# Output projection inside the attention loop of a graph-and-mixer layer on one core

## The chip, the cores and the metric

The kernel runs on one core of one Trainium2 chip. The metric is the time of one execution in device microseconds. Before the change the median of three runs is 1399.31 us (1399.07 to 1401.28). Whatever is under 0.2% of that cannot be told from no change.

## The reference, cut to what matters

The input has 1250 rows of 512 numbers (padded here to ten tiles of 128 rows) and a list of 21250 edges. After a layer norm, three parts are added to the rows: a graph network with four experts, linear attention with eight heads, and a feed-forward network with sixteen experts. The change touches the attention, the gate of the graph experts, and the start of the graph's neighbour sums:

```
xn = layernorm(x)
gates = softmax(xn @ gate_W + gate_b); the two largest of 4 are chosen, with their gate values
q, k, v = split(xn @ w_qkv) into 8 heads of 64;  q, k = elu(q) + 1, elu(k) + 1
kv = sum over rows of k (x) v
z  = 1 / (q . sum over rows of k + 1e-6)
attention = (q @ kv * z) @ w_out + b_out
aggr = (sum of xn over the incoming edges) / in-degree
x = x + graph(xn, gates) + attention;  then x = x + ffn(layernorm(x))
```

## The kernel before, in words

Each engine runs one list of instructions in written order, and semaphores tie the lists together. TensorE is PE in the rows, VectorE is DVE, ScalarE is ACT, GpSimd is POOL, and SyncE (SP) issues most loads. An instruction that waits holds up all that is behind it on its engine.

The change lies in the first quarter of the run. In the order of TensorE this is:

1. Transposes of the normed rows (L1519), then transposes of edge data (L1526 to L1530).
2. The gate logits of all ten tiles (`B[6]`, L1537, recorded at L1509 since all products go through `product`), then three small products that bring the bounds of the edge windows to one row (L1541).
3. Twelve query products, three column chunks of about 426 times four pairs of heads. After the first TensorE waits for `ex_max`, the gate's maximum on VectorE (L1055). The edges are also turned into a table of counts `AT`, 32 columns (one window) at a time: VectorE makes one-hot matrices (`hot_pair`, 24 instructions for two windows, L1083 and L1084), TensorE multiplies them (`window_pair`, L1552), ScalarE copies the counts out (L761). There are twenty pairs; six stand among the query products, ten in the next stage, four among the output rows.
4. For each of ten tiles a K product, a V product and a window pair. ELU plus one is computed as max(x, 0) + min(exp(x), 1): one exponential on ScalarE, a minimum (L1077) and a combined maximum and add (L1078) on VectorE.
5. Four K-V sums over all rows, one per pair of heads (`B[6]`, `B[7]`). VectorE copies each out (L1109, L1110) into `KVB` and `KS`, the latter with eight columns, one per head.
6. Denominators of chunks 0 and 1 (`KS` by the queries), each followed on VectorE by an add and a reciprocal over 8 rows (L1115, L1116). Chunk 2 follows after loop step 1.
7. The attention loop, twelve steps. A step multiplies the queries by `KVB`, and broadcasts the reciprocals to the head's rows with the 8-row mask `heads`. ScalarE copies the broadcast out (`at_factor`, L798), VectorE multiplies (`at_whole`, L1136), ScalarE takes the high part (`at_high`, L787), and VectorE the low part (`at_low`, L1121).
8. Ten output rows, twelve products each (high and low parts by high and low weights). VectorE adds each to `X` (L1144). The weights `WO` are loaded when K and V are done, and split on ScalarE (L791) and VectorE (L1127).
9. The aggregation, ten tiles: counts to rows (`count_rows`, L1642), neighbour sums from high and low parts (`summed`, L1660), transposes (L1676). It waits for the residuals of all rows, for `XN_H` (ScalarE, L804) and `XN_L` (GpSimd, L585), and for counts copied by ScalarE (`aconv`, L835) after VectorE has signalled `at_ready` (L1173). Before this signal VectorE computes the ranks of the rows within their experts (L1149 to L1154).

Beside this, GpSimd adds the output bias to all ten tiles of `X` in one instruction (L580). VectorE goes from the gate's maximum straight on to softmax and choice (L1057 to L1072), and only then to the first one-hot matrices. Later stages (expert layers, slots, feed-forward) are not touched.

Of the kernel before, what the change touches and what calls it, by code (L numbers as in the profile page):

```python
# [23 lines left out]
ACT = mybir.ActivationFunctionType  # L24
# [56 lines left out]
def program(nc, x, src, dst, gate_w, gate_b, wl, bl, wr, w_qkv, w_out, b_out, ffn_gate, ffn_bias,  # L81
# [57 lines left out]
    KS = here("KS", [P, HP, 2 * HP], F32)  # L139
    heads = here("heads", [2 * HP, HP, P], F32)  # L140
    den = here("den", [2 * HP, NP], F32)
# [67 lines left out]
    place[0] = W20  # L209
    aconv = [here(f"aconv{i}", [P, NT, P], F32R) for i in range(2)]  # L210
    aconv_low = here("aconv_low", [P, NT, P], F32R)
# [63 lines left out]
    def sem(name):  # L275
# [6 lines left out]
        "q_pe", "q_exp", "q_done", "k_pe", "k_exp", "k_done", "v_pe", "v_done", "kv_pe", "kv_done",  # L282
# [240 lines left out]
    def _(pool):  # L523
        done = [0]

        def link(ins):
# [39 lines left out]
        link(pool.memset(heads[:, :, :], 1.0))  # L566

        link(pool.affine_select(out=heads[:, :, :], in_=heads[:, :, :], compare_op=ALU.is_ge, fill=0.0,
                                base=0, pattern=[[P, HP], [1, P]], channel_multiplier=-P // 2))
        link(pool.affine_select(out=heads[:, :, :], in_=heads[:, :, :], compare_op=ALU.is_ge, fill=0.0,  # L570
                                base=P // 2 - 1, pattern=[[-P, HP], [-1, P]], channel_multiplier=P // 2))
        pool.wait_ge(S["bounds_out"], 1)
        for h in range(HP):
# [4 lines left out]
        pool.wait_ge(S["small_in"], 16 * 3)  # L578
        pool.wait_ge(S["xn_done"], NT)
        pool.tensor_tensor(X[:, :, :], X[:, :, :], bo[:, :].unsqueeze(1).to_broadcast([P, NT, D]), ALU.add)\  # L580
            .then_inc(S["bias_added"], 1)
# [162 lines left out]
    def _(act):  # L744
# [9 lines left out]
        act.wait_ge(S["ex_max"], 1)  # L754
        act.activation(lg[:, :, 0:GE], lg[:, :, 0:GE], ACT.Exp).then_inc(S["ex_exp"], 1)

# [6 lines left out]

        for n in range(12):
            c, w = CHUNKS[n // KD]
            act.wait_ge(S["q_pe"], n + 1)
            if n >= 2:
                act.wait_ge(S["q_done"], n - 1)
            act.activation(expo[n % 2][:, 0:w], B[n % 2][:, 0:w], ACT.Exp).then_inc(S["q_exp"], 1)
            if n in PAIR_AFTER_Q:  # L770
                window_pair(PAIR_AFTER_Q[n])
        for i in range(NT):
# [5 lines left out]
            act.activation(expo[i % 2][:, :], B[2 + i % 2][:, :], ACT.Exp).then_inc(S["k_exp"], 1)  # L778
# [10 lines left out]
        act.wait_ge(S["kv_pe"], HP)  # L789
        act.wait_ge(S["wqkv_in"], 32)  # L790
        act.activation(WO[1][:, :, :], WO[0][:, :, :], ACT.Copy).then_inc(S["wo_h"], 1)  # L791
        for n in range(12):
# [6 lines left out]
            if n >= 1:  # L799
                at_high(n - 1)  # L800
        at_high(11)
        for n in range(NT):

            act.activation(XN_H[:, n, :], XN[:, n, :], ACT.Copy).then_inc(S["xn_h"], 1)  # L804
        for i in sorted(PAIR_AFTER_O):
            window_pair(PAIR_AFTER_O[i])
# [25 lines left out]
        act.wait_ge(S["o_pe"], NT)  # L832
# [140 lines left out]
    def _(dve):  # L973
# [8 lines left out]
        def normalise(dest, round):  # L982
# [18 lines left out]
            for i in range(NT):  # L1001
# [45 lines left out]
        dve.wait_ge(S["small_in"], 16 * 3)  # L1047
        dve.wait_ge(S["lg_pe"], NT)
        dve.wait_ge(S["mix_setup"], 1)
        link(dve.tensor_tensor(lg[:, :, 0:GE], B[6][:, 0:NT * GE].rearrange("p (t e) -> p t e", e=GE),  # L1050
                               gb[:, :].unsqueeze(1).to_broadcast([P, NT, GE]), ALU.add))
        link(dve.tensor_reduce(lt[:, 0, :], lg[:, :, 0:GE], AX.X, ALU.max))
        link(dve.tensor_tensor(lg[:, :, 0:GE], lg[:, :, 0:GE], lt[:, 0, :].unsqueeze(2).to_broadcast([P, NT, GE]),
                               ALU.subtract))
        dve.sem_inc(S["ex_max"], 1)  # L1055
        dve.wait_ge(S["ex_exp"], 1)
        link(dve.tensor_reduce(lt[:, 1, :], lg[:, :, 0:GE], AX.X, ALU.add))  # L1057
        link(dve.reciprocal(lt[:, 2, :], lt[:, 1, :]))
        link(dve.tensor_tensor(lg[:, :, 0:GE], lg[:, :, 0:GE], lt[:, 2, :].unsqueeze(2).to_broadcast([P, NT, GE]),
                               ALU.mult))  # L1060
        for i in range(NT):
            last = dve.max(top8[:, i, :], lg[:, i, :])
        link(last)
        for i in range(NT):
            last = dve.max_index(idx8[:, i, :], top8[:, i, :], lg[:, i, :])
        link(last)
        link(dve.tensor_copy(idxf[:, :, :], idx8[:, :, :]))
        for k in range(GSEL):
            link(dve.tensor_tensor(pick4[:, k, :, :], idxf[:, :, k:k + 1].to_broadcast([P, NT, GE]),
                                   io8[:, 0:GE].unsqueeze(1).to_broadcast([P, NT, GE]), ALU.is_equal))  # L1070
        link(dve.tensor_tensor(M4[:, 0:NT, :], pick4[:, 0, :, :], pick4[:, 1, :, :], ALU.add))
        link(dve.tensor_tensor(coef[:, :, :], M4[:, 0:NT, :], lg[:, :, 0:GE], ALU.mult))  # L1072


        def feature(n, dest, e_tile, bank, exp_sem, done_sem):
            dve.wait_ge(S[exp_sem], n + 1)
            link(dve.tensor_scalar(e_tile, e_tile, 1.0, None, ALU.min))  # L1077
# [18 lines left out]
        hot_pair(0)  # L1096
        for n in range(12):
            (c, w), j = CHUNKS[n // KD], n % KD
            feature(n, QT[:, j, c:c + w], expo[n % 2][:, 0:w], B[n % 2][:, 0:w], "q_exp", "q_done")
            if n in PAIR_AFTER_Q:  # L1100
                hot_pair(PAIR_AFTER_Q[n] + 1)
        for i in range(NT):
            feature(i, K[:, i, :], expo[i % 2][:, :], B[2 + i % 2][:, :], "k_exp", "k_done")
            hot_pair(PAIR_AFTER_KV[i] + 1)
        for h in range(HP):
            dve.wait_ge(S["kv_pe"], h + 1)
            b = B[6 + h % 2]
            for m, r in enumerate((slice(0, 64), slice(64, P))):
                dve.tensor_copy(KVB[r, h, r], b[r, r])  # L1109
                last = dve.tensor_copy(KS[r, h, 2 * h + m:2 * h + m + 1], b[r, P:P + 1])  # L1110
            last.then_inc(S["kv_done"], 1)
        def denominators(chunk):
            c, w = CHUNKS[chunk]
            dve.wait_ge(S["den_pe"], chunk + 1)
            link(dve.tensor_scalar(den[:, c:c + w], B[4 + chunk % 2][0:2 * HP, 0:w], 1e-6, None, ALU.add))  # L1115
            dve.reciprocal(den[:, c:c + w], den[:, c:c + w]).then_inc(S["den_done"], 1)  # L1116
# [7 lines left out]
        denominators(0)  # L1124
        denominators(1)
        dve.wait_ge(S["wo_h"], 1)
        dve.tensor_tensor(WO[2][:, :, :], WO[0][:, :, :], WO[1][:, :, :].bitcast(F32), ALU.subtract).then_inc(S["wo_l"], 1)  # L1127
        for n in range(12):
            (c, w), h = CHUNKS[n // HP], n % HP

            if n == HP:
                denominators(2)
# [4 lines left out]
            if n >= 1:  # L1137
                at_low(n - 1)
        at_low(11)
        for i in range(NT):  # L1140
            dve.wait_ge(S["o_pe"], i + 1)
            if i == 0:
                dve.wait_ge(S["bias_added"], 1)
            dve.tensor_tensor(X[:, i, :], X[:, i, :], B[4 + i % 2][:, :], ALU.add).then_inc(S["o_done"], 1)  # L1144
            if i in PAIR_AFTER_O and PAIR_AFTER_O[i] + 1 < NW // 2:
                hot_pair(PAIR_AFTER_O[i] + 1)


        link(dve.tensor_tensor(M4[:, 0:NT, :], M4[:, 0:NT, :], valid[:, :].unsqueeze(2).to_broadcast([P, NT, GE]), ALU.mult))  # L1149
        link(dve.memset(pref4[:, 0, :], 0.0))  # L1150
        for i in range(1, NT):
            link(dve.tensor_tensor(pref4[:, i, :], pref4[:, i - 1, :], M4[:, i - 1, :], ALU.add))
        link(dve.tensor_tensor(M4[:, NT, :], pref4[:, NT - 1, :], M4[:, NT - 1, :], ALU.add))
        dve.sem_inc(S["gm_sel"], 1)  # L1154
        dve.wait_ge(S["win_done"], NW)
        long = dve.value_load(bounds_i[0:1, LONG:LONG + 1], min_val=0, max_val=ETP)
        with dve.If(long > 0):
            more = dve.alloc_register("dve_more")
            dve.reg_mov(more, 1)
            with dve.Fori(0, NW) as w:  # L1160
                at = dve.value_load(bounds_i[0:1, bass.ds(w + NW, 1)], min_val=VISITS, max_val=ETP - 1)
                end = dve.value_load(bounds_i[0:1, bass.ds(w + 2 * NW, 1)], min_val=VISITS, max_val=ETP - 1)
                with dve.If(end > at):
                    with dve.Fori(at, end) as t:
                        m = dve.snap(more, min_val=1, max_val=NW * ET)
                        one_hots(0, 0, bass.ds(t, 1), bass.ds(w, 1)).then_inc(S["lhot_ready"], 1)
                        dve.wait_ge(S["long_pe"], m)
                        part = AT[:, :, bass.ds(w * WIN, WIN)]
# [783 lines left out]
```

## Time and profile before

| what | value |
|---|---|
| median of three runs | 1399.31 us |
| the profiled execution: time, span | 1401.73 us, 1400.0 us |
| busy: TensorE, VectorE, ScalarE, GpSimd | 1285.5, 709.7, 428.9, 251.5 us |
| mean granted clock of TensorE | 0.948 of full speed |
| busy TensorE within 210 to 245 us, clock | 34.99 us, 0.61 |

The rows that follow further down give busy time, waits, single instructions and the chain that ended last. Busy TensorE time is not peak work: at half clock (0.50 in the rows) the same product takes twice as long and the engine is as busy as before. A step of the chain of waits gives the time that the work took on the path, without its overlap with the next; these are the prices used. A float32 product shows as two instructions.

### The profile page before, as it was taken

The numbers are of one execution on the slowest core, as the hardware profiler recorded it, in microseconds if no ns is written. First come the engines' busy times: TensorE is split into PE (matmuls) and PEld (weight loads), VectorE is DVE, ScalarE is ACT, GpSimd is POOL, SyncE is SP. The second block draws the span as 40 slices with busy tenths as digits, with TensorE's granted clock in tenths as the row PEclk, the third lists the DMA queues.
The fourth block names the chain that finished last, engine by engine and source line by source line (L and its number), as shares of the span: only waits on it lengthen the run. The fifth ranks groups of instructions, "written<-read, shape, count | busy, mean of one in ns | idle before, by whom it ended". The sixth has DMA issues, their size and how long they took to land.

```text
span 1400.0 us, 20256 instructions
## 1 busy us (share of the span) xinstructions
PE 1285.5 (92%) x6004; PEld 984.1 (70%) x6005; DVE 709.7 (51%) x1884; ACT 428.9 (31%) x760; POOL 251.5 (18%) x295
## 2 busy tenths in 40 slices
PE   5799999989898998999899989598999999999994
PEld 4454452678786886888678868376877888887883
DVE  5797765747463354235422432646364455436552
ACT  2022212235343233224322322422252243225431
POOL 2300000304102201320132002202721111111111
PEclk8599996999998998999999999799999999999998
DMA  9500000063424423451333443205673355336522
GB/s 352 208 1 1 1 31 0 1 212 119 137 72 133 119 79 117 102 139 65 114 97 84 139 147 72 86 10 150 193 237 68 54 136 140 57 61 187 167 48 35
DMA packets 71812, 145.94 MB, mean 104 GB/s; under 512 B 11555, under 2 KB 12289, under 8 KB 71749
## 3 DMA queue, kind: packets, MB, share of 16 engines
q1 hardware_dynamic: 54212, 99.39, 21.0%
q0 software_dynamic: 17536, 45.77, 15.6%
q8 instruction: 32, 0.52, 0.2%
q14 instruction: 32, 0.25, 0.1%
HBM read 86.47 MB, written 58.67 MB: 104 GB/s over the span
## 4 chain that ended last, share of the span: by engine, by line
PE 67%; DMA 12%; DVE 7%; issue 7%; POOL 4%; ACT 1%; POOLq 1%; DVEq 1%; SPq 0%; ACTq 0%
PE B L1867 19%; PE B L1717 15%; PE B L1509 15%; PE B L1724 6%; DMA own<-hidden,idxO 5%; PE B L1660 3%; PE B L1803 3%; PE B L1552 2%; DMA xg<-slots 2%; POOL slots L712 1%; POOL chosen_ids L602 1%; PE B L1848 1%; PE B L1743 1%; DMA out_rows<-y,y_tok 1%; PE B L1909 1%
## 5 line engine op out<-in xcount | busy, mean ns | idle before, releaser
L1867 PE MATMUL B<-GUWH,xtH 128*128 (+1 forms) x344 | 145.0, 422 | 0.8 <-DVE xtL L1342 0.8
L703 POOL DMA_INDIRECT out_rows<-y,y_tok x44 | 68.6, 1558 | 380.0 <-ACT y L938 370.0
L1867 PE MATMUL B<-GUWL,xtH 128*128 (+1 forms) x344 | 136.7, 397 | 0.0
L1867 PE MATMUL B<-GUWH,xtL 128*128 (+1 forms) x344 | 136.6, 397 | 0.0
L1308 DVE SCALAR_TENSOR_TENSOR owtL<-B,owtH 128x512 fp32r<-128x512 f32 x21 | 14.5, 692 | 145.3 <-ACT owtH L863 145.3
L1084 DVE TENSOR_SCALAR key<-iota_key,keyT,neg_win 128x320 bf16<-128x320 int16 x240 | 87.8, 366 | 0.0
L1660 PE MATMUL B<-GH,conv 128*128 128x512 f32 x210 | 81.9, 390 | 0.0
L1660 PE MATMUL B<-GL,conv 128*128 128x512 f32 x210 | 81.8, 389 | 0.0
L1867 PE MATMUL B<-DNWH,htH 128*128 x176 | 75.3, 428 | 1.7 <-DVE htL L1342 1.7
L1867 PEld LDWEIGHTS B<-GUWH,xtL 128*128 128x128 f32 x344 | 65.1, 189 | 15.8
L1293 DVE TENSOR_TENSOR tr<-B,b 128x512 f32<-128x512 f32 x40 | 27.7, 691 | 92.6 <-PE B L1717 91.4
L1867 PEld LDWEIGHTS B<-GUWH,xtH 128*128 128x128 f32 x344 | 65.2, 190 | 12.6 <-DVE xtL L1342 0.9
L1867 PEld LDWEIGHTS B<-GUWL,xtH 128*128 128x128 f32 x344 | 65.3, 190 | 11.2
L1083 DVE TENSOR_SCALAR low<-iota_low,lowT 128x128 bf16<-128x128 int16 x240 | 61.0, 254 | 22.6 <-PE B L1552 21.4
L938 ACT ACTIVATE y<-B,y_gate 128x512 f32<-128x512 f32 x44 | 30.3, 689 | 135.4 <-PE B L1867 87.4
L822 ACT ACTIVATE hsXH<-XT 128x512 fp32r<-128x512 f32 x40 | 25.2, 631 | 150.5 <-PE B L1717 148.6
L1509 PE MATMUL B<-WQKV,XT 128*128 128x512 f32 x160 | 70.3, 592 | 0.0
L1867 PE MATMUL B<-DNWL,htH 128*128 x176 | 69.6, 395 | 0.0
L1867 PE MATMUL B<-DNWH,htL 128*128 x176 | 69.6, 395 | 0.0
L1803 PE MATMUL B<-ident,raw 128*128 128x128 f32 x432 | 64.5, 274 | 2.6 <-DVE DNWL L1342 1.5
L1717 PE MATMUL B<-W1H,hsXH 128*128 128x512 f32 x160 | 63.3, 396 | 2.8 <-DVE hsAL L1184 1.8
L1803 PEld LDWEIGHTS B<-ident,raw 128*128 128x128 f32 x432 | 52.6, 141 | 18.9 <-DVE DNWL L1342 3.6
(361 smaller groups left out, 2906.2 us busy)
## 6 DMA issues: line engine op xcount, KB each, us to landing
raw<-in_L_ffn_expert_gate_up SPq DMA_DIRECT2D x16, 1024.0 KB, 5.4
slots<-fill SPq DMA_DIRECT2D x5, 2112.0 KB, 19.6
hidden<-tr SPq DMA_DIRECT2D x40, 256.0 KB, 2.0
xg<-slots SPq DMA_DIRECT2D x34, 264.0 KB, 2.7
raw<-in_L_ffn_expert_down SPq DMA_DIRECT2D x8, 1024.0 KB, 5.7
counts<-astage SPq DMA_DIRECT2D x10, 648.0 KB, 3.1
W1R<-in_L_gnn_Wr SPq DMA_DIRECT2D x4, 1024.0 KB, 5.9
W1R<-in_L_gnn_Wl SPq DMA_DIRECT2D x4, 1024.0 KB, 8.8
```

What stands on the lines that cost most here:

```text
L703: pool.indirect_dma_start(out=out, out_offset=bass.IndirectOffsetOnAxis(ap=y_tok[:, 0:1], axis=0), in_=y[:, :], in_offset=None, compute_op ...
L938: act.activation(y[:, :], B[5][:, :], ACT.Copy, scale=y_gate[:, 0:1]).then_inc(S["y_done"], 1)
L1083: dve.tensor_scalar(low1[:, slot, v, :], iota_low[:, :], lowT[:, tile_col], None, ALU.is_equal)
L1084: return dve.tensor_scalar(key1[:, slot, v, :], iota_key[:, :], keyT[:, tile_col], neg_win[:, window], ALU.subtract, ALU.is_equal)
L1293: dve.tensor_tensor(tr[i % 2][:, :], B[2 - i % 2][:, :], b1[:, :], ALU.add).then_inc(S["t_done"], 1)
L1509: last = pe.matmul(bank, a, b, start=start and n == 0, stop=stop and n == len(todo) - 1)
L1552: last = pe.matmul(b, low1[:, lo_h, v, :], key1[:, lo_h, v, :], start=v == 0, stop=v == VISITS - 1)
L1660: last = pe.matmul(bank, counts[:, a, :], part[:, a, :], start=not begun and a == 0 and m == 0, stop=stop and a == NT - 1 and m == 1, skip ...
L1717: last = pe.matmul(B[2 - i % 2][:, :], rows[2 * (k // KD) + a][:, k % KD, :], W1[b][:, k, :], start=k == 0 and n == 0, stop=k == K2 - 1 an ...
L1724: last = pe.matmul(B[0][:, :], rows[a][:, k, :], W2[b][:, k0 + k, :], start=not begun and k == 0 and n == 0, stop=begun and k == KD - 1 an ...
L1803: last = pe.transpose(B[PREP_BANKS[q % PRING]][:, cols(k)], raw[:, q, cols(k)], ident[:, :])
L1867: last = pe.matmul(bank, rows[a][:, k, :], weights[b](k), start=k == 0 and n == 0, stop=k == KD - 1 and n == 2)
```

## The change

- The gate logits go into `B[5]` and stand among the query products, one tile after each of products 1 to 10; the window bounds come after product 0. The maximum follows the last query feature on VectorE. Its exponential on ScalarE follows the query features, softmax and choice follow output rows 6 and 7, and the ranks row 8.
- ELU plus one becomes max(x, 0) + exp(-relu(-x)): two passes on ScalarE (`below`) and one on VectorE.
- The bias is added by VectorE tile by tile between the copies of the K-V sums; the weight split moves there too.
- `KS` gets three shifted copies of its columns, so that all three chunks accumulate in one bank: 72 rows, chunk by chunk at rows 0, 32 and 64. One add and one reciprocal do for all; the mask `heads` has 72 rows and three versions, built by GpSimd when K and V are done, in the place of the query and key weights.
- Output rows 0 to 5 stand in the loop after steps 5, 6, 7, 9, 10 and 11. The last four window pairs stand after the denominators and after rows 1, 3 and 5; their one-hots on VectorE at steps 2, 7 and 10.
- `at_ready` is signalled before the last residual. The aggregation's first tile takes its sum before its counts, and waits for the residuals only after it.

```diff
-PAIR_AFTER_Q = {2 * p + 1: p for p in range(6)}
+PAIR_AFTER_Q = {2: 0, 4: 1, 6: 2, 8: 3, 10: 4, 11: 5}
-PAIR_AFTER_O = {2 * q + 1: 16 + q for q in range(4)}
+BIAS_AFTER_KV = ((0, 1, 2), (3,), (4, 5, 6), (7, 8, 9))
+PAIR_AFTER_O = {1: 17, 3: 18, 5: 19}
+PAIR_AFTER_DEN = 16
+O_AFTER = {5: 0, 6: 1, 7: 2, 9: 3, 10: 4, 11: 5}
+DEN = 72
...
+        pool.wait_ge(S["k_pe"], NT)
+        pool.wait_ge(S["v_pe"], NT)
+        link(pool.memset(heads[:, :, :, :], 1.0))
+        link(pool.affine_select(out=heads[:, :, :, :], in_=heads[:, :, :, :], compare_op=ALU.is_ge, fill=0.0,
+                                base=0, pattern=[[32 * P // 2, 3], [P, HP], [1, P]], channel_multiplier=-P // 2))
...
+        def below(dest, bank, n, done_sem):
+            act.activation(dest, bank, ACT.Relu, scale=-1.0).then_inc(S["ft_relu"], 1)
+            act.wait_ge(S["ft_relu"], n + 1)
+            act.activation(dest, dest, ACT.Exp, scale=-1.0).then_inc(S[done_sem], 1)
...
-        act.wait_ge(S["kv_pe"], HP)
         act.wait_ge(S["wqkv_in"], 32)
         act.activation(WO[1][:, :, :], WO[0][:, :, :], ACT.Copy).then_inc(S["wo_h"], 1)
+        window_pair(PAIR_AFTER_DEN)
...
+                of = 2 * h + m
+                last = dve.tensor_copy(KS[r, h, of:of + 2 * (DEN + 32) + 1:DEN + 32], b[r, P:P + 1].to_broadcast([64, 3]))
             last.then_inc(S["kv_done"], 1)
+            if h == 0:
+                dve.wait_ge(S["small_in"], 16 * 3)
+            for i in BIAS_AFTER_KV[h]:
+                last = dve.tensor_tensor(X[:, i, :], X[:, i, :], bo[:, :], ALU.add)
+            if h == 1:
+                dve.wait_ge(S["wo_h"], 1)
+                dve.tensor_tensor(WO[2][:, :, :], WO[0][:, :, :], WO[1][:, :, :].bitcast(F32), ALU.subtract)\
+                    .then_inc(S["wo_l"], 1)
...
+        dve.wait_ge(S["den_pe"], 1)
+        link(dve.tensor_scalar(den[:, :], B[5][0:DEN, 0:CHUNKS[0][1]], 1e-6, None, ALU.add))
+        dve.reciprocal(den[:, :], den[:, :]).then_inc(S["den_done"], 1)
...
+        hot_after = {2: 17, 7: 18, 10: 19}
         for n in range(12):
...
             if n >= 1:
                 at_low(n - 1)
+            if n - 1 in O_AFTER:
+                residual(O_AFTER[n - 1])
+            if n in hot_after:
+                hot_pair(hot_after[n])
         at_low(11)
+        gating = {6: gate_softmax, 7: gate_choice, 8: expert_ranks}
+        for i in range(O_AFTER[11], NT):
+            residual(i)
+            if i in gating:
+                gating[i]()
...
+        for chunk, (c, w) in enumerate(CHUNKS):
+            for h in range(HP):
+                last = pe.matmul(B[5][0:DEN, 0:w], KS[:, h, chunk * DEN:(chunk + 1) * DEN], QT[:, h, c:c + w],
+                                 start=chunk == 0 and h == 0, stop=chunk == 2 and h == HP - 1, skip_group_check=True)
+        last.then_inc(S["den_pe"], 1)
+        window_pair(PAIR_AFTER_DEN)
...
+            if n == 0:
+                pe.wait_ge(S["mix_setup"], 2)
+                pe.wait_ge(S["den_done"], 1)
+            product(B[2 + n % 2][:, 0:w], [(heads[:, n // HP, h, :], den[:, 0:w])]).then_inc(S["at_pe"], 1)
+            if n in O_AFTER:
+                output_rows(O_AFTER[n])
...
         for i in range(NT):
-            count_rows(i)
+            if i == 0:
+                pe.wait_ge(S["conv_done"], 1)
+            else:
+                count_rows(i)
...
+            if i == 0:
+                pe.wait_ge(S["o_done"], NT)
+                count_rows(0)
+            else:
                 transpose_rows_out(i - 1)
```

## Rows read from the trace of the kernel before

**Rows 1.** Chain of waits, 0 to 360 us: start, length, engine, line, count.
```profile
66.07 8.30 PE B L1509 x16
74.37 1.63 PE B L1552 x12
76.00 5.72 PE B L1509 x16
...
105.39 6.87 PE B L1509 x16
...
271.61 5.52 PE B L1509 x24
...
284.35 0.69 DVE X L1144
...
290.20 2.39 PE B L1642 x10
292.59 6.28 PE B L1660 x20
298.87 1.07 PE B L1642 x10
299.94 4.64 PE B L1660 x20
```

**Rows 2.** Stretches: length, busy PE, PEld, DVE, ACT, POOL; then clock, DMA, GB/s.
```profile
36.00:41.00 5.00, 5.00 (x28) 4.90 (x28) 0.00 (x0) 0.00 (x0) 0.00 (x0) 0.50 1.06 388
74.00:83.00 9.00, 9.00 (x41) 5.23 (x39) 7.77 (x30) 2.89 (x6) 0.00 (x0) 1.00 0.01 2
206.83:210.48 3.65, 3.65 (x9) 1.18 (x9) 3.62 (x3) 0.53 (x1) 0.00 (x0) 1.00 0.00 0
217.00:244.00 27.00, 27.00 (x33) 7.79 (x32) 12.25 (x19) 7.79 (x16) 0.00 (x0) 0.51 0.00 0
```

**Rows 3.** Timeline of all engines, 0 to 70 us: start, length, engine, line, operation.
```profile
11.08 0.62 POOL L570 TENSOR_SCALAR_AFFINE_SELECT heads<-heads 8x512 f32<-8x512 f32 x1
...
24.79 15.85 PE L1509 MATMUL B<-gw,XT 128*128 128x4 f32 x80
...
28.65 0.15 DVE L1037 TENSOR_TENSOR lohi<-lohi 40x1 f32<-40x1 f32 x1
...
43.17 10.96 POOL L580 TENSOR_TENSOR X<-X,bo 128x5120 f32<-128x5120 f32 x1 [0.25 <-POOL V L574]
43.57 10.62 DVE L1053 TENSOR_TENSOR lg<-lg,lt 128x40 f32<-128x40 f32 x1
```

**Rows 4.** Waits of TensorE, 0 to 365 us: total, times, longest.
```profile
PE B L1509 <- DVEq L1055: 7.3, 1, 7.3
PE B L1642 <- ACT aconv L835: 5.9, 1, 5.9
```

**Rows 5.** The load of the query, key and value weights: issue and landing.
```profile
L394 SPq DMA_DIRECT2D WQKV<-in_L_mix_w_qkv x1: 480/480/480, 6.2 to 6.2; - x1
...
DMA to landing us min/median/max: 14.6/14.6/14.6
```

**Rows 6.** Timeline of VectorE, 186 to 300 us.
```profile
189.69 0.25 DVE L1083 TENSOR_SCALAR low<-iota_low,lowT 128x128 bf16<-128x128 int16 x1 [2.12 <-PE B L1552]
...
194.93 0.20 DVE L1109 COPY KVB<-B 64x64 f32<-64x64 f32 x1
...
204.70 2.82 DVE L1116 RECIPROCAL den<-den 8x428 f32<-8x428 f32 x1
...
210.74 2.22 DVE L1127 TENSOR_TENSOR WOL<-WO,WOH 128x2048 fp32r<-128x2048 f32 x1
...
253.16 1.38 DVE L1084 TENSOR_SCALAR key<-iota_key,keyT,neg_win 128x320 bf16<-128x320 int16 x1
```

**Rows 7.** Timeline of TensorE: the denominators of chunks 0 and 1.
```profile
201.00 5.90 PE L1509 MATMUL B<-QT,KS 128*8 128x428 f32 x16 [0.69 <-DVE KS L1110]
```

**Rows 8.** Timeline of GpSimd: the low parts of the normed rows.
```profile
246.89 12.54 POOL L585 TENSOR_TENSOR XN_L<-XN,XN_H 128x512 fp32r<-128x512 f32 x10 [192.75 <-ACT XN_H L804]
```

More of the change, by code:

```diff
@@ L565, in _ @@
         link(pool.memset(KS[:, :, :], 0.0))
[L566 to L571, printed above, removed]
         pool.wait_ge(S["bounds_out"], 1)
@@ L576, in _ @@
         pool.sem_inc(S["mix_setup"], 1)
[L578 to L581, printed above, removed]
+        pool.wait_ge(S["k_pe"], NT)
[3 more added lines that the diff above has]
+                                base=0, pattern=[[32 * P // 2, 3], [P, HP], [1, P]], channel_multiplier=-P // 2))
+        link(pool.affine_select(out=heads[:, :, :, :], in_=heads[:, :, :, :], compare_op=ALU.is_ge, fill=0.0,
+                                base=P // 2 - 1, pattern=[[-32 * P // 2, 3], [-P, HP], [-1, P]],
+                                channel_multiplier=P // 2))
+        pool.sem_inc(S["mix_setup"], 1)
         for i in range(NT):
@@ L1109, in _ @@
                 dve.tensor_copy(KVB[r, h, r], b[r, r])
-                last = dve.tensor_copy(KS[r, h, 2 * h + m:2 * h + m + 1], b[r, P:P + 1])
+                of = 2 * h + m
+                last = dve.tensor_copy(KS[r, h, of:of + 2 * (DEN + 32) + 1:DEN + 32], b[r, P:P + 1].to_broadcast([64, 3]))
             last.then_inc(S["kv_done"], 1)
[L1112 to L1116, printed above, removed]
+            if h == 0:
[6 more added lines that the diff above has]
+                    .then_inc(S["wo_l"], 1)
+        last.then_inc(S["bias_added"], 1)
         def at_low(n):
@@ new lines, in windows_done @@
+        def windows_done():
+            dve.wait_ge(S["win_done"], NW)
+            with dve.If(long > 0):
+                more = dve.alloc_register("dve_more")
+                dve.reg_mov(more, 1)
+                with dve.Fori(0, NW) as w:
+                    at = dve.value_load(bounds_i[0:1, bass.ds(w + NW, 1)], min_val=VISITS, max_val=ETP - 1)
+                    end = dve.value_load(bounds_i[0:1, bass.ds(w + 2 * NW, 1)], min_val=VISITS, max_val=ETP - 1)
+                    with dve.If(end > at):
+                        with dve.Fori(at, end) as t:
+                            m = dve.snap(more, min_val=1, max_val=NW * ET)
+                            one_hots(0, 0, bass.ds(t, 1), bass.ds(w, 1)).then_inc(S["lhot_ready"], 1)
+                            dve.wait_ge(S["long_pe"], m)
+                            part = AT[:, :, bass.ds(w * WIN, WIN)]
+                            dve.tensor_tensor(part, part, B[6][:, 0:WC].rearrange("p (a w) -> p a w", a=NT), ALU.add)\
+                                .then_inc(S["long_done"], 1)
+                            dve.wait_ge(S["long_done"], m)
+                            dve.reg_add(more, more, 1)
+            dve.sem_inc(S["at_ready"], 1)
@@ new lines, in expert_ranks, with residual @@
+        def expert_ranks():
+            link(dve.tensor_tensor(M4[:, 0:NT, :], M4[:, 0:NT, :], valid[:, :].unsqueeze(2).to_broadcast([P, NT, GE]), ALU.mult))
+            link(dve.memset(pref4[:, 0, :], 0.0))
+            for i in range(1, NT):
+                link(dve.tensor_tensor(pref4[:, i, :], pref4[:, i - 1, :], M4[:, i - 1, :], ALU.add))
+            link(dve.tensor_tensor(M4[:, NT, :], pref4[:, NT - 1, :], M4[:, NT - 1, :], ALU.add))
+            dve.sem_inc(S["gm_sel"], 1)
+        def residual(i):
+            if i == NT - 1:
+                windows_done()
+            dve.wait_ge(S["o_pe"], i + 1)
+            if i == 0:
+                dve.wait_ge(S["bias_added"], 1)
+            dve.tensor_tensor(X[:, i, :], X[:, i, :], B[4 + i % 2][:, :], ALU.add).then_inc(S["o_done"], 1)
@@ L1149, in _ @@
[L1149 to L1168, printed above, removed]
-                        dve.tensor_tensor(part, part, B[6][:, 0:WC].rearrange("p (a w) -> p a w", a=NT), ALU.add)\
-                            .then_inc(S["long_done"], 1)
-                        dve.wait_ge(S["long_done"], m)
-                        dve.reg_add(more, more, 1)
@@ L1652, in count_rows @@
                 for a in range(NT):
-                    one(aconv_low, a, False)
+                    last = one(aconv_low, a, False)
+                if i == 0:
+                    last.then_inc(S["ag_low_pe"], 1)
             one(aconv[i % 2], NT - 1, True).then_inc(S["ar_pe"], 1)
```

161 lines of the change are left out of this document (76 added, 85 removed).

## The prediction

> **What bounds the kernel now.** I read the page, then the busy time by stage, the waits of TensorE, the timeline of all engines at the start, and the chain of waits. Everything that the change touches lies before the second aggregation tile, whose products start at 299.94 us [rows 1]; what follows only moves along. TensorE is the bound almost throughout: in the query stage it is busy 9.00 of 9.00 us at clock 1.00 [rows 2]. Three places lose time. The gate logits, 80 instructions with 4 moving columns, take 15.85 us at the start, at clock 0.50 [rows 2, 3]. Then TensorE waits 7.3 us for VectorE's gate maximum [rows 4]: its subtract of 128x40 shows 10.62 us, inside GpSimd's one bias add of 10.96 us [rows 3]. In the attention loop TensorE is busy 27.00 of 27.00 us, but at clock 0.51 [rows 2]. And after the last output row it waits 5.9 us for the count copies [rows 4].
>
> **Query stage.** Before, the first logit starts at 24.79 and K's first product at 105.39 [rows 1, 3]: 80.6 us. The weights for the queries were issued at 6.2 and landed 14.6 us later [rows 5], so the first query product can start at 24.9, where the logits stood. Its work: 12 query products at 5.72/2 us, 34.3; six window pairs at 1.63, 9.8 [rows 1]; 80 logit instructions; 0.5 us for the window bounds. A logit costs between 0.107 us (ten short matmuls in 1.07 us [rows 1]) and 0.20 (15.85/80 [rows 3]); I take the first, 8.6 us in all, because pairs mixed with query products ran at clock 1.00 [rows 2]. Waits: the bounds are ready at 28.8 [rows 3], product 0 ends at 27.7, so 1.1 us. The first hot pair, 5.24 us on VectorE [rows 6], starts only after feature 1, about 35.3, and ends at 40.6; TensorE arrives at 36.8 and needs 1.63 us, so 2.3 are lost, and 0.6 more at the last pair. The sum is 57.2 us: K starts at 82.1, 23.3 us earlier. Logits, their maximum and the bias leave the path; ScalarE's second pass per feature (some 0.6 us, 22 times) and VectorE's lost minimum both lie beside TensorE, whose nine-microsecond period leaves either slack. The K and V stage keeps its 8.5 us per tile. Two waits for the maximum are new: V's second product, and ScalarE's list, where K's exponentials stand behind it. The maximum follows a hot pair and a feature on VectorE, near 88.8; V's second product comes at 94.0, and K's first feature, late by 3.5 us, lets the next hot pair end at 96.8, before TensorE wants it at 97.5. Both are hidden, the second by 0.7 us.
>
> **K-V sums and denominators.** What is late next is VectorE. Its last hot pair moves from 189.69 to 166.4 and would end at 171.6. But GpSimd now builds the head mask there, three operations over 3x512 elements, about 1.2 us ahead of it. One over 512 took 0.62 us [rows 3], so they take 1.9 us (by the instruction) to 5.6 (by the element), and a hot-pair operation beside a GpSimd operation took 1.38 us instead of about 0.3 [rows 6]. The delay is 0.7 to 4.4 us; I take 3.4, nearer the price by element. Behind it VectorE must pass sixteen small copies (some 0.15 us each, 2.4), seven of the ten bias adds (0.6 each, by the 0.69 of a like row [rows 1]: 4.2) and the weight split (2.22 [rows 6]) before TensorE has its last key sum: the denominators start at 183.8, not 201.00 [rows 7]. The pauses are too short for what is put into them, 6.1 of the 23.3 us go here. Then come 24 instructions at 5.90/16 (8.8 us [rows 7]) and one window pair: the loop starts at 194.2, before at 206.9 (201.00 plus 5.90). One add of 0.6 and one reciprocal of 2.82 us [rows 6] end at 196.1, so the first broadcast waits 1.0 us. The two other reciprocals were hidden; the third denominator product, 3.0 us, leaves the loop.
>
> **Loop and output rows.** Work: 12 steps at 1.83 us (two in 3.65 us at full clock [rows 2]), 22.0; ten rows at 5.52/2, 27.6; three pairs, 4.9 [rows 1]. VectorE now has hot pairs among the loop's products. At step 2 the pair stands before product 3, which step 5 needs: VectorE is done 7.9 us after step 2, TensorE has 3.66 us to do, so 4.3 lost. At step 7 row 3 needs a low part behind the pair: 9.0 against 6.4, 2.6 lost. At step 10 row 6: 10.2 against 9.0, 1.2 lost. With the 1.0 above that is 63.6 us: the last row ends at 257.8. Before it took from 206.9 to 284.35 [rows 1].
>
> **Start of the aggregation.** GpSimd's low parts (12.54 us [rows 8]) start with row 6, and the gate's choice now stands on VectorE beside them. An operation with two SBUF inputs waits there like the 10.62 us one [rows 3]; with five such the low parts end 13.5 us after row 6 began, row 9 11.0 after. Only then come the last but one residual, the expert ranks and the copy, the 5.9 us chain of before [rows 4]. The gap is 8.4 us; without holding, 2.8. Then the first tile's sum, its counts, a new wait of 1.3 us (its counts must be copied out before the next counts, which the sum covered before) and 1.07: 4.64 + 1.07 + 1.3 + 1.07, plus the 3.0 us of cold clock that the same start cost before (2.39 + 6.28 against 1.07 + 4.64 [rows 1]). The second tile starts at 277.2 instead of 299.94: 22.7 us.
>
> GpSimd's list now waits for K and V ahead of the mask; behind it stand only the low parts, wanted 70 us later. SP's loads and stores wait for the same rows and come earlier by as much; the load of the output weights has over ten microseconds of room.
>
> **The clock.** Right after a paced hot pair two query products took 8.30 us instead of 5.72 [rows 1]: 2.6 us. The first pair stays paced, so I charge this again, and half of it, 1.3, at the denominators, where TensorE idles some 7 of 11 us: 22.7 less 3.9 is 18.8. The profiled run took 1401.73 us, 1400.0 of it span, and is 2.4 above the median; taken from each it leaves 1382.9 for a run like it and 1380.5 for the median.
>
> **Two rules of the Trainium skill.** That GpSimd holds VectorE is seen in the 10.62 and 1.38 us rows [rows 3, 6]. The Trainium skill, SBUF — State Buffer, section SBUF: two separate sides, says the port pair is locked for a whole instruction, also by an operation that only writes; no row here shows the latter. By it the mask's fill holds VectorE too, and the 3.4 us stay; by rows alone two of three operations would hold it, some 1.2 us less. The other: the loop was busy throughout and yet at 0.51 [rows 2]. The Trainium skill, TensorE: Matmul & The Clock Gate, Part 1, says that sustained activity releases the slow clock and idling brings it back; by that rule alone the loop would have been fast before, so the trace disagrees, and the new mask with 72 rows instead of 8 need not decide it as the rule would have it.
>
> **Rivals.** First, the clock is low longer. For: the loop's pattern was granted 0.51. A step at half clock costs 27.00/33x4, 3.3 us, 1.4 more. Until row 0 that is six steps, less the two hidden in the 4.3 us wait: 5.7 us, 1386.2. If instead query products 0 to 2 and their logits run at half, that is 10.3 us more, of which the waits of 1.1 and 2.3 and the 2.6 already charged take up 6.0: 4.3, 1384.8; both, 1390.5. Against: the first two steps after the denominators ran at full clock [rows 2], and output rows follow from step 5. Second, GpSimd holds VectorE little (short mask operations, gate operations slipping between): 2.7 and 5.6 us back, 1372.2, and without the cold spells 1368.3. Against: the 10.62 us row. Third, slower: the logits, which ran at 0.50, keep the clock at half through the whole query stage. Its 52.7 us of work double, K starts near 127 instead of 105.4, 22 us late; with the other parts, which about cancel, 1422. It decides once half clock covers more than about 22 of the 52.7 us beyond the forecast. Against: window pairs among query products ran at 1.00. The change not doing what it says: if the query weights came late the first product could not move up, but they landed at 20.8.
>
> **Chances.** My sum 0.52; clock low longer 0.27; little holding 0.14; slower 0.05; a gain eaten up by several of these, 0.02. Range 1368 to 1392, which takes in the first two rivals; the last two cases lie outside. A measurement of this kernel tells about 0.2% from no change. Faster by more 0.92, within 0.03, slower 0.05.
>
> **What would show it.** Right: K's first product near 82; a VectorE hot pair stretched beside GpSimd's mask; denominators near 184, loop near 194, one wait of about 4 us at step 5; a gap of 8 us before the aggregation; its second tile near 280. Wrong: a clock of 0.5 over most of the query stage or the loop; gate operations at 0.2 us beside the low parts; denominators before 180.

## The result and the profile after

The changed kernel takes 1378.94 us (median of four runs, 1377.66 to 1379.18), the kernel before took 1400.3 on the same chip: on record as a ratio of 0.9861, 95% interval 0.984 to 0.9883 (the quotient of the two medians, 0.9847, lies inside it). Forecast were 1380.5 us, and 1382.9 for a run like the profiled one; the profiled run took 1379.03 us, 1377.3 of it span, 22.7 less than before.

The chain of waits of the changed kernel, 0 to 360 us (start, length, engine, line, count), answers to [rows 1]:

```profile
82.63 6.87 PE B L1538 x16
...
184.30 10.52 PE B L1628 x24
...
259.55 1.23 DVE pick L1101
...
263.50 0.69 DVE X L1182
267.13 1.17 ACT aconv L843
268.34 7.35 PE B L1700 x20
...
277.98 1.30 PE B L1680 x10
279.29 4.60 PE B L1700 x20
```

K's first product starts 22.8 us earlier than before, the denominators 16.7, the second aggregation tile 20.65. The first scatter of the chosen rows starts 20.67 us earlier, so the gain reaches the next stage whole. Of the other 2.0 us that the profiled run gained, 1.5 come where the list of chosen rows is loaded back (5.48 us, before 7.01); the change does not touch that load.

TensorE's waits of the changed kernel, 0 to 350 us (total, times, longest), answer to [rows 4]:

```profile
...
PE B L1700 <- ACT aconv L843: 6.4, 1, 6.4
PE B L1538 <- DVE expo L1190: 4.7, 1, 4.7
PE B L1538 <- DVE QL L1138: 4.2, 2, 3.1
PE B L1628 <- DVE KS L1123: 3.6, 1, 3.6
PE B L1538 <- DVE KS L1123: 2.7, 1, 2.7
...
PE B L1538 <- DVE den L1143: 1.3, 1, 1.3
PE B L1680 <- ACT astage L849: 1.2, 1, 1.2
PE B L1572 <- DVEq L1046: 1.0, 1, 1.0
```

The 7.3 us wait for the gate's maximum is gone. All waits listed are new or moved. Each of them but the one of 1.3 us shrank or went in one of the experiments, the one of 1.0 us only with the logits in a block. The stretches of the changed kernel, with the columns of [rows 2] (the clock is the third number from the end):

```profile
25.00:42.00 17.00, 15.13 (x65) 8.33 (x66) 12.04 (x49) 4.13 (x8) 0.59 (x4) 1.00 1.06 385
42.00:82.00 40.00, 39.88 (x193) 25.63 (x191) 30.15 (x125) 13.59 (x27) 0.00 (x0) 1.00 0.31 113
...
184.30:188.50 4.20, 4.20 (x7) 1.56 (x8) 1.87 (x3) 0.00 (x0) 0.00 (x0) 0.59 0.00 0
...
210.10:216.00 5.90, 5.87 (x12) 3.75 (x13) 2.63 (x5) 1.53 (x3) 0.00 (x0) 0.52 0.00 0
216.00:230.00 14.00, 14.00 (x58) 9.28 (x56) 6.53 (x21) 3.57 (x8) 0.00 (x0) 1.00 0.00 0
...
233.20:236.30 3.10, 3.10 (x8) 2.48 (x9) 1.55 (x3) 0.02 (x1) 0.00 (x0) 0.52 0.00 0
...
268.40:274.00 5.60, 5.60 (x14) 4.39 (x15) 0.00 (x0) 1.05 (x1) 0.04 (x1) 0.52 1.05 399
```

The query stage is at full clock, and so is the loop apart from short stretches. Each stretch near 0.5 (1.2 of 2.4 GHz), called a cold stretch in what follows, stands behind one of the waits above: the 3.6, the 4.7, the 3.1 and the 6.4 us one. Before, the clock was low in 27 us of uninterrupted work.

### The profile page after: what moved, and what is told of

It is laid out like the page before. It is cut to its first block, busy times and chain, and to the rows that moved or that the text cites. A ratio compares the mean times of both kernels' runs of the same rounds, so it can differ in the third digit from the quotient of the medians.

```text
span 1377.3 us, 20264 instructions
## 1 busy us (share of the span) xinstructions
PE 1255.1 (91%) x6004; PEld 975.5 (71%) x6005; DVE 693.8 (50%) x1868; ACT 441.2 (32%) x782; POOL 243.8 (18%) x294
## 4 chain that ended last, share of the span: by engine, by line
PE 64%; DMA 12%; DVE 9%; issue 7%; POOL 4%; ACT 1%; DVEq 1%; POOLq 1%; SPq 0%; ACTq 0%
PE B L1919 19%; PE B L1769 15%; PE B L1538 10%; PE B L1776 6%; DMA own<-hidden,idxO 5%; PE B L1700 4%; PE B L1855 3%; DMA xg<-slots 2%; PE B L1584 2%; POOL chosen_ids L606 1%; POOL slots L716 1%; PE B L1900 1%; PE B L1795 1%; DMA out_rows<-y,y_tok 1%; DVE key L1063 1%
## 5 line engine op out<-in xcount | busy, mean ns | idle before, releaser
L831 ACT ACTIVATE hsXH<-XT 128x512 fp32r<-128x512 f32 x40 | 25.3, 631 | 149.0 <-PE B L1769 147.1
```

## The experiments

Each edit starts from the changed kernel unless the text says otherwise. The runs stood on other chips, beside the kernel before (1396.8 to 1397.8 us there) but not beside the changed kernel. So ratios to the kernel before are compared with 0.9861, and stages by the trace. Each kernel has one trace.

**Logits in a block.**

```diff
+        for i in range(NT):
+            gate_logits(i)
+        window_bounds()
         for n in range(12):
...
-            elif n <= NT:
-                gate_logits(n - 1)
```

> The changed kernel with its 80 logit instructions back in one block, ahead of the first query product, and the window bounds right behind them; the maximum stays behind the last query feature. Theory: a block of short products runs at half clock (0.56 in that stretch before) and hands the low clock on. The block takes 15.85 us instead of 10 times 0.81 among the query products, the 1.0 us wait for the bounds goes: K's first product moves from 82.5 to 89 if full speed is back at once, and towards 95 if the first query products also run slow, as before (5.98 us against 3.14). Time 1386 to 1391. Rival: what made the logits slow was the load beside them or the wait for the maximum, not their standing together; then the block takes some 8 us, K starts near 82, 1378.

1389.21 us, ratio 0.9943 (0.9926 to 0.996), about 11 us more. Timeline of TensorE, then the first stretch:

```profile
25.23 14.87 PE L1538 MATMUL B<-gw,XT 128*128 128x4 f32 x80
...
40.52 11.05 PE L1538 MATMUL B<-XT,WQKV 128*128 128x428 f32 x24
...
93.12 7.03 PE L1538 MATMUL B<-WQKV,XT 128*128 128x512 f32 x16
```
```profile
25.00:41.00 16.00, 16.00 (x92) 15.80 (x92) 3.86 (x16) 0.00 (x0) 0.00 (x0) 0.59 1.06 385
```

The same 80 instructions cost 8.1 us among the query products and 14.87 in a block, and three products behind the block take 11.05 us, where a product takes 3.14 at full clock. K starts 10.6 us later. The load beside them is as heavy in both kernels (385 GB/s) and TensorE does not wait for the maximum here, so the rival falls.

**The maximum early, then with a long GpSimd operation.** Both start from the kernel with the block of logits.

```diff
         for n in range(12):
...
+            if n == 0:
+                gate_maximum()
...
             if n == 0:
...
+                pe.wait_ge(S["ex_max"], 1)
...
+        pool.tensor_tensor(X[:, :, :], X[:, :, :], fill[:, 0:D].unsqueeze(1).to_broadcast([P, NT, D]), ALU.add)\
+            .then_inc(S["bias_added"], 1)
```

> The kernel with the logits in one block, and the gate's maximum ahead of the first query feature, TensorE waiting for it before its second query product, as before; the bias stays on VectorE in ten adds late. Theory: the 7.3 us wait of before was GpSimd's one add holding the maximum, not the maximum: it takes some 2 us beside a product at half clock of 6 us, so no wait over 0.5 us comes back: 1388 to 1391, as with the logits in a block alone. Rival: the wait belongs to the maximum's chain itself, and 5 to 7 us come back: 1394 to 1397.

> The same, and GpSimd adds a row of zeros to all ten tiles in one operation where it added the bias before. Theory: the maximum's subtract waits for the end of that add, and TensorE waits some 7 us before its second query product; the clock stays low for longer: K's first product moves to where it was before, 103 to 106: 1396 to 1400. Rival: the two do not hold each other; then 1388 to 1391.

1390.69 us, ratio 0.9946 (0.9924 to 0.9967), and 1398.74 us, ratio 1.0012 (1.0002 to 1.0023). TensorE waits for the maximum behind its first query product. The last two lines of the edit are the second kernel's alone; `fill` holds zeros. The subtract of the maximum, in the timelines of VectorE of the first and of the second kernel, with GpSimd's add and TensorE's wait in the second:

```profile
43.50 0.20 DVE L1081 TENSOR_TENSOR lg<-lg,lt 128x40 f32<-128x40 f32 x1
```
```profile
43.48 10.65 DVE L1085 TENSOR_TENSOR lg<-lg,lt 128x40 f32<-128x40 f32 x1
...
43.11 10.96 POOL L577 TENSOR_TENSOR X<-X,fill 128x5120 f32<-128x5120 f32 x1 [0.25 <-POOL V L572]
```
```profile
PE B L1544 <- DVEq L1087: 7.2, 1, 7.2
```

The maximum itself was harmless: alone the subtract takes 0.20 us and TensorE does not wait; beside the add it takes 10.65, and a wait of 7.2 us is back. That add costs 8 us. Together with the block of logits it moves K's first product from 82.5 to 102.0 us, 19.5 of the 22.8 us that the change won there; the rest was not taken apart.

**Mask of 8 rows.**

```diff
-            product(B[2 + n % 2][:, 0:w], [(heads[:, n // HP, h, :], den[:, 0:w])]).then_inc(S["at_pe"], 1)
+            product(B[2 + n % 2][:, 0:w], [(heads[0:2 * HP, 0, h, :], den[0:2 * HP, 0:w])]).then_inc(S["at_pe"], 1)
```

> The changed kernel with only 8 rows of mask and reciprocals in each broadcast product, those of the first column chunk for all (so the attention of the other chunks is scaled by wrong reciprocals). Theory: the 1.83 us of a step before came with the operand of 8 rows, and 72 rows took it away: a step (two products) goes from 1.45 back to 1.83 us at full clock, twelve times, of which about four lie in waits for VectorE: plus 3 us, 1382; if the clock then also falls to half as it did before, a step takes 3.4 us and it is 1385 to 1395. Rival: the height is nothing, the steps were slow because the third denominator and the later reciprocals lay among them: steps stay at 1.45 us, 1379.

1390.68 us, ratio 0.9954 (0.9937 to 0.997). This total can't be read: the changed attention sent rows to other experts, and the feed-forward network ran one tile more (45 against 44). The loop can. Timeline of TensorE, then three stretches:

```profile
201.84 0.98 PE L1538 MATMUL B<-den,heads 8*128 8x428 f32 x2
...
203.67 0.98 PE L1538 MATMUL B<-den,heads 8*128 8x428 f32 x2
204.58 1.40 PE L1538 MATMUL B<-QT,KVB 128*128 128x426 f32 x2
```
```profile
199.00:204.50 5.50, 5.50 (x13) 1.77 (x12) 2.73 (x5) 2.48 (x5) 0.00 (x0) 1.00 0.01 3
204.50:213.90 9.40, 6.58 (x9) 1.79 (x8) 7.46 (x29) 2.06 (x4) 0.00 (x0) 0.53 0.00 1
...
218.70:234.00 15.30, 14.75 (x54) 8.01 (x53) 8.04 (x28) 4.09 (x9) 0.00 (x0) 1.00 0.00 0
```

A step is back at 1.83 us at full clock (201.84 to 203.67), as in [rows 2], and the clock falls at 204.6, in the midst of work without a wait, while the changed kernel stays at 1.00 through the same steps (199.0 to 204.5). So the height of the operand sets the price of a step, and in this trace 8 rows brought the low clock. They did not keep it: from 218.7 on, with output rows between the steps, the clock is back at 1.00. In the kernel before no output rows stood between the steps and the clock stayed low for 27 us. The change put 72 rows and output rows into the loop together, and 72 rows without the output rows were not run, so their shares are not known. From the first broadcast to the first sum this kernel takes 73.1 us (198.22 to 271.32), the changed one 69.9. What in the hardware makes it so, no run shows.

**Bias adds and weight split behind the last copy; mask behind it.** Two kernels; the last three lines are the second one's, and the split moves in the first like the adds.

```diff
-            for i in BIAS_AFTER_KV[h]:
-                last = dve.tensor_tensor(X[:, i, :], X[:, i, :], bo[:, :], ALU.add)
...
+        for i in range(NT):
+            last = dve.tensor_tensor(X[:, i, :], X[:, i, :], bo[:, :], ALU.add)
...
-        pool.wait_ge(S["k_pe"], NT)
-        pool.wait_ge(S["v_pe"], NT)
+        pool.wait_ge(S["kv_done"], HP)
```

> The changed kernel with the ten bias adds and the weight split behind the last copy of the K-V sums instead of between the copies. Theory: they stand in TensorE's way there. The third sum still waits for the hot pair, the denominators start at 181.4 instead of 184.3, the idle time before them shrinks from 3.6 to under 1 us, and with it the stretch at half clock behind it (1.7 us) may go; VectorE has 8.6 us of work beside 8.85 us of denominators: 1374 to 1376. Rival: the work does not fit there, the add and the reciprocal come later by what the denominators come earlier: 1379.

> The changed kernel with GpSimd building the mask only after the last copy of the K-V sums. Theory: the mask held VectorE: the hot pair goes from 8.05 back to 5.24 us, and the denominators start 2.8 us earlier, near 181.5: 1376; the mask is ready near 187, before the loop. Rival: VectorE's delay was made up in the waits behind it; the denominators move by less than 1 us: 1379.

1376.21 us, ratio 0.9853 (0.9837 to 0.987), and 1375.54 us, ratio 0.985 (0.9834 to 0.9867): each ratio lies within the interval of the changed kernel's, so the totals tell nothing and the traces decide. Denominators in the timeline of TensorE of the changed kernel, of the first and of the second; then the last two K-V sums and the denominators of the kernel with the mask of 8 rows, whose instructions are those of the changed kernel up to the loop:

```profile
184.30 10.51 PE L1628 MATMUL B<-QT,KS 128*72 128x428 f32 x24 [3.61 <-DVE KS L1123]
```
```profile
180.57 8.81 PE L1626 MATMUL B<-QT,KS 128*72 128x428 f32 x24 [0.70 <-DVE KS L1123]
```
```profile
183.05 8.81 PE L1627 MATMUL B<-QT,KS 128*72 128x428 f32 x24 [3.61 <-DVE KS L1122]
```
```profile
177.11 6.38 PE L1538 MATMUL B<-V,K 128*128 128x129 f32 x40 [2.73 <-DVE KS L1123]
...
185.76 8.81 PE L1628 MATMUL B<-QT,KS 128*72 128x428 f32 x24 [2.28 <-DVE KS L1123]
```

From the first K-V sum to the start of the denominators the changed kernel takes 16.1 us (168.21 to 184.30), the first kernel 12.9 (167.71 to 180.57), the second 13.3 (169.80 to 183.05): 3.2 and 2.8 us of waiting are won, and both rivals fall. The 1.7 us of low clock in the denominators go as well, but they cannot be put down to the edits: with the mask of 8 rows the same work shows them too at 8.81 us, since there the cold stretch falls on the last two sums (6.38 us, in the changed kernel 5.05), ahead of a wait that hides it. So from the first sum to the first broadcast the unedited stage takes 30.2 or 28.5 us, the edited ones 25.3 and 25.7. In the second kernel the hot pair is back at 0.25 us for an operation [rows 6], the wait of 2.7 us is gone, while the 3.6 us wait stays and yet the clock does not fall: in this trace that wait by itself did not bring the low clock. What decides where a cold stretch falls, no run shows.

**One-hots of pair 17 at step 5.**

```diff
-        hot_after = {2: 17, 7: 18, 10: 19}
+        hot_after = {5: 17, 7: 18, 10: 19}
```

> The changed kernel with the one-hots of pair 17 made on VectorE at step 5 of the loop, when output rows follow, and no longer at step 2. Theory: the 4.7 us wait of step 5 comes from their place alone, and the 5.9 us at clock 0.52 behind it come from that wait. Both go, the pair's product finds its one-hots ready behind row 1: 4.7 and some 2.8 us, 1371.5. Rival: VectorE is late in the loop as a whole, the wait comes back before pair 17 or row 1, and 1 to 3 us are won: 1376 to 1378.

1370.87 us, ratio 0.9801 (0.9777 to 0.9825), 8 us less. Waits of TensorE:

```profile
PE B L1538 <- DVE QL L1138: 4.8, 3, 3.1
...
PE B L1584 <- DVE key L1063: 0.4, 1, 0.4
```

The 4.7 us wait is gone, 0.6 (in the first line, 4.2 before) and 0.4 came for it, and the clock stays at 1.00 behind step 5. From the first broadcast to the first sum it takes 63.0 us against 69.9.

**Gate in VectorE's pauses.**

```diff
+        gating = {2: gate_softmax, 4: gate_choice, 6: expert_ranks}
         for i in range(NT):
...
+            if i in gating:
+                gating[i]()
             hot_pair(PAIR_AFTER_KV[i] + 1)
```

> The changed kernel with softmax, choice and expert ranks in VectorE's pauses at K and V tiles 2, 4 and 6, not behind output rows 6 to 8. Theory: beside GpSimd's low parts each of these operations waits for one of them, and their chain makes the gap of 6.4 us before the aggregation. Without them the residual of row 8 follows its row, and the low parts end last, 1.3 us after the last row; the cold start of the first sum (7.35 us against 4.6) goes with the gap if the clock fell for its sake: 5 to 8 us, 1371 to 1374. The pauses hold them: a tile has 2.4 us of VectorE idle. Rival: they do not fit there, pairs of the K and V stage come late and take back 2 to 4 us; or the gap stays over 5 us since the low parts themselves are held.

1372.39 us, ratio 0.9818 (0.9797 to 0.9838), 6 us less. Timeline of TensorE and of GpSimd:

```profile
264.77 0.47 PE L1700 MATMUL B<-XN_H,aconv 128*128 128x512 f32 x1 [1.58 <-POOL XN_L L589]
...
252.07 12.55 POOL L589 TENSOR_TENSOR XN_L<-XN,XN_H 128x512 fp32r<-128x512 f32 x10 [79.48 <-ACT XN_H L815]
```

The gap is 1.6 us, not 6.4, and no wait came in the K and V stage. The low parts take 12.55 us with nothing of the gate beside them, as with it (12.54): the time that the two held each other was VectorE's alone. The first sum ran at full speed; the next tile was the slow one, so not the whole cold start was won.

**Counts first.**

```diff
             if i == 0:
-                pe.wait_ge(S["conv_done"], 1)
-            else:
-                count_rows(i)
+                pe.wait_ge(S["o_done"], NT)
+            count_rows(i)
...
-            if i == 0:
-                pe.wait_ge(S["o_done"], NT)
-                count_rows(0)
-            else:
+            if i >= 1:
                 transpose_rows_out(i - 1)
```

> The changed kernel with the aggregation's first tile in the old order: its counts before its sum, both behind the residuals. Theory: the new order wins nothing here and adds a wait of 1.2 us between the first two tiles, since the gap ends with the copy of the counts in either case: from the end of the gap to the second tile's sum 9.7 us (as before) instead of 10.9, 1377.7. Rival: the new order is needed, because the last residual comes later than the copies; then the old one starts up to 1 us later.

1376.09 us, ratio 0.985 (0.9829 to 0.987). Chain of waits:

```profile
266.64 1.17 ACT aconv L843
...
277.38 4.64 PE B L1700 x20
```

From the copy to the second sum it takes 10.7 us, in the changed kernel 12.2, and the wait of 1.2 us between them is gone. By the traces this part of the change lost 1.4 us; by time alone it can't be told from nothing.

**ELU as before.**

```diff
-            act.activation(dest, bank, ACT.Relu, scale=-1.0).then_inc(S["ft_relu"], 1)
...
+            act.activation(dest, bank, ACT.Exp).then_inc(S[done_sem], 1)
...
+            link(dve.tensor_scalar(e_tile, e_tile, 1.0, None, ALU.min))
```

> The changed kernel with ELU plus one as before: one exponential on ScalarE, a minimum and a combined operation on VectorE. Theory: the one pass and the other both lie beside TensorE, whose tiles of 8.5 us leave either slack: 1377 to 1380, no wait of TensorE in the query or K and V stage over 0.5 us that was not there. Rival: the minimum (0.6 us a feature) makes the window pairs late, some 0.5 us a tile, 4 to 6 us in all: 1383 to 1385.

1379.13 us, ratio 0.9869 (0.9851 to 0.9886): no change, and in the K and V stage no wait that was not there.

**All in one, twice.** The main lines of the first kernel, then those by which the second differs from it. `PAIR_AFTER_DEN` is 17 here.

```diff
+        pool.wait_ge(S["kv_pe"], 2)
...
+            if n == 0:
                 hot_pair(0)
...
+            b = B[h]
...
+        hot_pair(PAIR_AFTER_DEN)
...
+            if i == 6:
                 windows_done()
...
+        hot_after = {5: 18, 9: 19}
...
+        window_pair(PAIR_AFTER_DEN - 1)
```
```diff
+        for n in range(NT):
+
+            act.activation(XN_H[:, n, :], XN[:, n, :], ACT.Copy).then_inc(S["xn_h"], 1)
         window_pair(PAIR_AFTER_O[O_AFTER[11]])
...
+            if i == 7:
                 windows_done()
...
+            count_rows(i)
+            if i == 0:
+                pe.wait_ge(S["xn_l"], NT)
```

> All in one: gate as in the early-gate kernel; bias adds in the pauses of K and V; K-V sums into four banks of their own, so that no copy holds them; the mask built while the third sum runs; pair 16 between the sums and the denominators, one-hots of pair 17 and the weight split beside the denominators; pairs 18 and 19 at steps 5 and 9, their products behind rows 1 and 5; the first hot pair after feature 0; the windows' signal before row 6. Theory, by the waits of the changed kernel: first pair 2.4, loop begun 6.9 earlier, step 5 with its cold stretch 7.5, rows 3 and 6 with theirs 5.6, gap and cold start 8: 30 us, 1347 to 1351. Rival: as the waits go VectorE or the low parts become the bound at the end of the rows and the clock falls elsewhere: 1355 to 1365.

> The all-in-one kernel, with ScalarE's high parts of the normed rows ahead of its copies of the last window pair (so the low parts on GpSimd start 3.3 us earlier), the windows' signal before row 7, and the first tile's counts ahead of its sum, beside the low parts. Theory: the low parts (12.5 us) end the wait of 2.7 us before the first sum, which then starts cold (6.4 us against 4.6); with them earlier both go, and the counts leave the place between the sums: the second tile's sum starts near 243.6 instead of 249.4; 5 to 6 us less than the all-in-one kernel, about 1345. Rival: the earlier low parts hold VectorE's last low part of the queries, row 6 waits, and the rows end as much later: 1349 to 1351.

1350.7 us, ratio 0.9658 (0.9638 to 0.9678), and 1350.41 us, ratio 0.9668 (0.9651 to 0.9685). The first beats both kernels: some 47 us less than before, 28 less than the change. TensorE's waits in the stages that it touches, then VectorE's copies beside the mask on GpSimd, which take what they take alone [rows 6]:

```profile
...
PE B L1698 <- POOL XN_L L588: 2.7, 1, 2.7
...
PE B L1678 <- ACT astage L850: 1.2, 1, 1.2
```
```profile
168.85 0.20 DVE L1137 COPY KVB<-B 64x64 f32<-64x64 f32 x1
...
168.82 1.43 POOL L577 MEMSET heads<- 72x1536 f32 x1 [138.37 <-PE B L1538]
170.32 1.55 POOL L579 TENSOR_SCALAR_AFFINE_SELECT heads<-heads 72x1536 f32<-72x1536 f32 x1
```

The second won nothing more. Its time lies in the rival's range, but neither the theory nor the rival's reason was right. Its second tile's sum does start near 244.7 us, some 5 us earlier. But then ScalarE waits for a store, and TensorE for ScalarE (SyncE's issue of the stores first):

```profile
246.15 16.02 SPq L438 DMA_DIRECT2D counts<-astage  x3
```
```profile
258.33 1.09 ACT L850 ACTIVATE astage<-B 128x512 f32<-128x512 f32 x2 [7.04 <-DMA counts<-astage]
...
259.52 2.37 PE L1678 MATMUL B<-ident_r,aconv 128*128 128x128 f32 x10 [2.98 <-ACT astage L850]
```

The stores of the counts go out on SP's queue behind the next weights and the stored rows, which are issued when the last output row is done; 190 to 400 GB/s run until about 258 us. The wait of 3.0 us and the cold start behind it (2.37 for the counts, and 6.14 for the sum) give the 5 us back: the fourth tile's sum starts at 261.9 us, in the first kernel at 262.3. That these loads, issued later, would keep them was not tried.

## Why the prediction was right, point by point

- **Query stage.** Forecast 57.2 us, measured 57.4 (25.19 to 82.63). A tile's logits took 0.81 us (forecast 0.86), the wait for the bounds 1.0 (1.1), the first hot-paced pair 3.9 against 1.63 (2.3 lost, as forecast).
- **K's start to the denominators.** Forecast 101.7 us, measured 101.7. The mask took 4.6 us, near the price by element, and the delay of the hot pair was 2.8 (3.4). Its fill, and two of the one-hot operations beside fill and first select, in the timelines of GpSimd and VectorE of the changed kernel:

```profile
166.09 1.37 POOL L578 MEMSET heads<- 72x1536 f32 x1 [134.62 <-PE B L1538]
```
```profile
166.93 0.59 DVE L1062 TENSOR_SCALAR low<-iota_low,lowT 128x128 bf16<-128x128 int16 x1 [2.37 <-PE B L1584]
...
167.52 1.62 DVE L1062 TENSOR_SCALAR low<-iota_low,lowT 128x128 bf16<-128x128 int16 x1
```

  The Trainium skill, SBUF — State Buffer, section SBUF: two separate sides, says the port pair that VectorE and GpSimd share is held for a whole instruction. The trace agrees: one-hots of 0.25 us took up to 1.62 beside the mask's selects, and the first took 0.59, until the end of the fill, which only writes. So the case for which the prediction had no row is shown here, for operations with one input. The section says too that VectorE's other pair never waits; the copies from PSUM at 0.20 to 0.23 us beside fill and selects, in the all-in-one kernel, fit that.
- **Denominators.** 24 instructions took 10.5 us instead of 8.8: a cold stretch of 1.7, charged with 1.3. That it fell here is luck: with the same work ahead, the kernel with the mask of 8 rows took 8.81.
- **Loop and rows.** Forecast 63.6 us, measured 65.6 (196.27 to 261.9), by errors that nearly cancel: luck, then. The step of 1.83 us was mis-sized: with 72 rows it took 1.45, 4.6 us less over twelve. The four waits came where they were forecast: 1.3, 4.7, 3.1 and 1.2, in sum 1.1 more than 9.1. What was left out are the cold stretches behind two of them, 5.9 us at 0.52 and 3.1 at 0.52: half of each, 4.5. Of the 2.0 us by which the stage was longer, 1.0 stays unexplained.
- **Gap.** 6.4 us, not 8.4. Four of the five operations that were to be held took 1.1 to 1.2 us each; the fifth came behind the low parts. These ended 12.7 us after row 6 began, not 13.5, the rows ended 0.4 later, and the chain from the last but one residual to the copied counts took 4.8, not the 5.9 of before.
- **Start of the aggregation.** Forecast 11.1 us with its cold start, measured 10.95.
- **The clock.** This step failed, in mechanism and place. The 2.6 us charged behind the first hot pair did not come, the stretch ran at 1.00; 4.5 came in the loop instead. The doubt about the rule of the Trainium skill (TensorE: Matmul & The Clock Gate, Part 1) was right: it has the clock released by sustained activity, and the products with 8 rows lost it without a pause, in the kernel before [rows 2] and in the experiment. The forecast drew no gain from that, since it took the old price of a step for the new one.
- **Third rival.** It did not come true, and one of its sums does not come out: 24.9 and 0.5 and twice 52.7 us put K's start at 130.8, not near 127.

The median came out 1.6 us under the forecast, the profiled run 3.9. Of these 3.9, 1.9 are the stages, which gave 20.65 us where 18.8 were forecast, and 2.0 came from outside them. The stages fit in part by luck: the step that was too dear (4.6 us) paid for cold stretches that were not charged (4.5), and the shorter gap (2.0) for the longer loop (2.0).

## What to carry to other kernels

A pause on an engine is worth what stands behind it there: the bias adds and the weight split cost 3.2 us between copies that TensorE waits for and, in the all-in-one kernel, brought no wait of TensorE in the pauses of other stages. Before pricing a stage by its old steps, ask what made them slow, since a change of an operand's height can change the price and the clock. When a stage is started earlier, look at which transfers it now meets.

## What the runs showed of the hardware that was not expected

- A broadcast product over 8 rows made a step of two products 1.83 us at full clock, and four such steps in a row were followed, without a wait, by a clock of 0.53; with output rows between them the clock was 1.00. Over 72 rows a step was 1.45 us, and the clock stayed at 1.00 through the same steps.
- Waits and cold stretches do not go one to one. In the changed kernel a wait of 2.7 us brought none and one of 3.6 us behind it 4.2 us at 0.59. With the mask of 8 rows, and the same instructions up to there, the 2.7 us wait brought it (6.38 us for the next two sums, 5.05 in the changed kernel) and the next wait none. Where the first wait was gone, the 3.6 us one brought none either.
- A GpSimd operation of 11 us held a VectorE operation of 0.20 us for 10.65, at a cost of 8 us of run time.
